# Two mixture-of-experts stages: how rows reach their expert's blocks, and who splits the weights

## What is computed

```python
w, sel = top_k(dist(y, centroid), 2)       # two experts for each token
w = softmax(w)
for e in range(8):
    h = silu(y @ Wg[e] + bg[e]) * (y @ W1[e] + b1[e])
    out += we[:, e:e+1] * (h @ W2[e] + b2[e])
```

## Time and profile before

| | |
|---|---|
| median of 3 runs | 1390.04 us (1389.5 to 1395.8) |
| the profiled execution | 1399.42 us |
| its span, first to last instruction | 1397.6 us, mean granted TensorE clock 0.809 |
| TensorE busy | 1033.1 us (74%) |
| VectorE busy | 731.0 us (52%) |
| ScalarE busy | 574.9 us (41%) |
| GpSimd busy | 429.5 us (31%) |

### The profile page before, as it was taken

How to read it: one execution, slowest core, us unless ns; L and a number is a source line. 1 busy time by engine, 2 the same in 40 slices (tenths; PEclk the granted TensorE clock), 3 DMA queues, 4 the chain that set the end, 5 groups by cost and what they waited for, 6 DMA issues and landing times. The chain is left out here.

```text
span 1397.6 us, 23299 instructions
## 1 busy us (share of the span) xinstructions
PE 1033.1 (74%) x7645; PEld 757.6 (54%) x7645; DVE 731.0 (52%) x1988; ACT 574.9 (41%) x1177; POOL 429.5 (31%) x462
## 2 busy tenths in 40 slices
PE   3899883569962787878665899999995556518990
PEld 2566553559951555554343566666663445418990
DVE  3467625466654656555253655655532455654553
ACT  1356532155532355445333354444441244324552
POOL 1144433513442111110143133333342241572332
PEclk9999965689985568775577899999997666658995
DMA  7111100111230111111030000111122430011113
GB/s 262 41 43 56 56 30 12 37 30 42 55 85 0 32 48 42 38 35 44 18 118 0 2 23 18 25 32 32 32 52 42 143 137 0 20 40 41 53 49 91
DMA packets 80293, 68.33 MB, mean 49 GB/s; under 512 B 6769, under 2 KB 72600, under 8 KB 79666
## 3 DMA queue, kind: packets, MB, share of 16 engines
q1 hardware_dynamic: 75666, 58.37, 14.6%
q0 software_dynamic: 4512, 8.47, 1.9%
HBM read 40.61 MB, written 26.59 MB: 48 GB/s over the span
## 5 line engine op out<-in xcount | busy, mean ns | idle before, releaser
L413 DVE TENSOR_REDUCE a_rowmax<-a_banks 128x4 f32<-128x1024 f32 (+1 forms) x112 | 137.0, 1223 | 109.4 <-PE a_banks L623 92.3
L507 ACT ACTIVATE a_probs<-a_banks 128x1024 f32<-128x1024 f32 x112 | 114.8, 1025 | 108.1 <-PE a_banks L609 88.6
L2133 POOL TENSOR_TENSOR a_both<-a_probs 128x512 f32<-128x512 f32 x64 | 81.8, 1278 | 193.5 <-ACT a_probs L2336 193.5
L1054 POOL DMA_INDIRECT acc<-m_result,m_yb x77 | 75.7, 983 | 156.3 <-DVE m_result L1346 82.0
L2336 ACT ACTIVATE a_probs<-a_banks 128x1024 f32<-128x1024 f32 x64 | 65.6, 1025 | 114.2 <-PE a_banks L2384 114.2
L2245 DVE TENSOR_REDUCE a_rowmax<-a_banks 128x4 f32<-128x1024 f32 x64 | 78.0, 1219 | 23.9 <-PE a_banks L2364 23.9
L1452 ACT ACTIVATE m_gate<-m_banks 128x352 f32<-128x352 f32 (+1 forms) x93 | 42.8, 460 | 104.8 <-PE m_banks L1639 87.3
L647 PE MATMUL a_banks<-a_probs,a_V 128*32 128x256 f32 x768 | 79.0, 495 | 5.6 <-ACT a_raw L500 4.9
L609 PE MATMUL a_banks<-a_QT,a_KT 25*128 25x256 f32 x384 | 59.6, 393 | 30.4 <-DVE a_rowmax L413 29.3
L1047 POOL DMA_INDIRECT rows<-m_yrow,m_idx x64 | 64.0, 1000 | 47.9 <-issue 22.9
L609 PEld LDWEIGHTS a_banks<-a_QT,a_KT 25*128 25x128 f32 x384 | 37.1, 232 | 67.9 <-issue 50.8
(11 more groups left out here) (347 smaller groups left out, 2854.7 us busy)
## 6 DMA issues: line engine op xcount, KB each, us to landing
rows<-fill SPq DMA_DIRECT2D x16, 520.0 KB, 4.6
a_factor<-recip_rows SPq DMA_DIRECT2D x32, 256.0 KB, 4.6
rows<-fill SPq DMA_DIRECT2D x15, 455.0 KB, 4.2
m_yb<-rows SPq DMA_DIRECT2D x77, 65.0 KB, 1.8
f_expert<-in_experts SPq DMA_DIRECT2D x16, 257.5 KB, 2.9
m_parts<-acc SPq DMA_DIRECT2D x16, 256.0 KB, 5.0
bias<-in_bias_zero SPq DMA_DIRECT2D x1, 3248.0 KB, 20.1
e_gu_lo<-in_gu SPq DMA_DIRECT2D x1, 2736.0 KB
```

The source lines that it names most:

```text
L413: nc.vector.reduce_max(o, src, AX).then_inc(rowmax_ready, 1)
L507: nc.scalar.activation(probs[h][:, k, :, :], ps[:, 4:6, :], ACT.Exp, scale=SCALE).then_inc(exp_done, 1)
L1054: nc.gpsimd.indirect_dma_start(acc.rearrange("k n d -> (k n) d"), bass.IndirectOffsetOnAxis(yb[b % YB][:, P:P + 1].bitcast(U32), 0), resul ...
L2133: nc.gpsimd.tensor_tensor(both[u % 4][:, :, :], p[:, :, 0, :], p[:, :, 1, :], ALU.add).then_inc(both_ready, 1)
```

## The change

`rows` is now laid out by partition and place: each token's normed row lies, once for each choice, where its tile has it, so SyncE stores them with 8 plain DMAs in each layer (2 for each run), and place 0 holds zeros. The fills in the attentions, the scatters of line 1047 and the loads of line 1006 are gone. A row has 129 words, without the place.

In their stead each block's list of pairs is worked out: VectorE finds each pair's block and its row in the block (`positions`), makes for each pair a one-hot row over the 128 rows of a block (`block_list`) and a product of its one-hot block with its own partition and place (`listed`), and TensorE multiplies and adds the two (32 small bfloat16 products, event `list`) so that each block's column holds, for each of its rows, the partition and the place of its pair. `indices` turns this into `idx` for gathers and `idx_out` for scatters (out of bounds where a block has no pair). The events `count`, `list` and `idx` take the place of `map`; in layer 0 they stand between slots 2 and 5, in layer 3 after the last run's routing.

GpSimd gathers each block by an indirect DMA (`gather`) and scatters its results as before. In slot r it first gathers item r + 5 (GA), with the wait that SyncE's loads had, then scatters item r-2. GpSimd also does the low parts of all split experts but layer 0's shared one, which VectorE keeps. In layer 0 the work items are now 10 shared tiles, the blocks with a shared tile after blocks 8, 17, 26 and 35, and 2 shared tiles; the splits come earlier in the events. `acc` has the layout of `rows`, so its loads read 4 rows of a partition in one run of 2 KB.

The diff, cut to its core:

```diff
-ROW = P + 2
+ROW = P + 1
+PLACES = 2 * TILES + 1
+NOWHERE = float(1 << 24)
...
+def shared_first_work(NB, lead, every, behind):
+
+    work = [("shared", t) for t in range(lead)]
+    t = lead
+    for b in range(NB):
+        work.append(("routed", b))
+        if b % every == every - 1 and t < TILES - behind:
+            work.append(("shared", t))
+            t += 1
+    return work + [("shared", u) for u in range(t, TILES)]
...
+             ("spot", 0), ("share", 0), ("split", 0), "slot", ("norm", 2), ("router", 2), ("one_hot", 1), ("split", 1), "slot",
+             ("score", 2), ("gap", 2), ("spot", 1), ("share", 1), ("split", 2), "slot", ("norm", 3), ("router", 3),
+             ("one_hot", 2), ("split", 3), "slot", ("score", 3), ("gap", 3), ("spot", 2), ("share", 2), ("one_hot", 3),
+             ("split", 4), "slot", ("spot", 3), ("share", 3), ("split", 5), ("split", 6), ("count", 0), "slot", ("list", 0),
+             ("list", 1), "slot", ("list", 2), ("list", 3), ("idx", 0)]
...
-    splits = {0: [0, 1, 2], 1: [3], 5: [4, 5], 6: [6, 7]}
+    splits = {0: [0, 1], 1: [2], 2: [3], 3: [4], 4: [5], 5: [6], 6: [7]}
...
-    events += [("send", RUNS - 1, 3), ("map", 0)]
+    events += [("count", 0)] + [("list", r) for r in range(RUNS)] + [("idx", 0)]
...
-    YB, RB = 8, 4
+    YB, RB, GA = 8, 4, 5
...
-            work = [("shared", t) for t in range(14)] + [("routed", b) for b in range(NB)] + [("shared", 14), ("shared", 15)]
+            work = shared_first_work(NB, 10, 9, 2)
...
-            sp.wait_ge(rows_sent, 16 * 2 * TILES)
-            sp.wait_ge(map_ready, 1)
-            own_wait(sp, st.sp_waited)
-            for b in range(NB):
-                n = sp.value_load(block_map[0:1, 1, b:b + 1], min_val=0, max_val=dispatch_rows(layer) // P - 1)
-                if b >= YB:
-                    sp.wait_ge(result_sent[(b - YB) % RB], 16 * ((b - YB) // RB + 1))
-                sp.dma_start(yb[b % YB][:, :], rows[n, :, :]).then_inc(block_loaded[b % YB], 16)
+            sp.dma_start(rows[:, 0, :], g.fill[:, :]).then_inc(rows_stored, 16)
+            for r in range(RUNS):
+                sp.wait_ge(copied, r + 1)
+                sp.wait_ge(share_ready, r + 1)
+                for k in range(2):
+                    first_place = 1 + k * TILES + r * RT
+                    sp.dma_start(rows[:, first_place:first_place + RT, :], yrow[k][:, tiles(r), :]).then_inc(rows_stored, 16)
             for k in range(RB):
                 sp.wait_ge(result_sent[k], 16 * len(range(k, NB, RB)))
             for r in range(RUNS):
                 for k in range(2):
-                    sp.dma_start(parts[r][:, k, :, :],
-                                 acc[k, r * RUN:(r + 1) * RUN, :].rearrange("(t p) d -> p t d", p=P)).then_inc(
-                        parts_loaded[r], 16)
+                    first_place = 1 + k * TILES + r * RT
+                    sp.dma_start(parts[r][:, k, :, :], acc[:, first_place:first_place + RT, :]).then_inc(parts_loaded[r], 16)
...
-            def send(r, some):
-                pool.wait_ge(idx_ready, r + 1)
-                pool.wait_ge(share_ready, r + 1)
-                pool.wait_ge(copied, r + 1)
-                pool.wait_ge(places_ready, 1)
-                pool.wait_ge(g.filled[layer], 16 * g.fill_parts)
-                for t in some:
-                    for k in range(2):
-                        c = (r * RT + t) * 2 + k
-                        nc.gpsimd.indirect_dma_start(rows.rearrange("n p c -> (n p) c"),
-                                                     bass.IndirectOffsetOnAxis(idx[:, c:c + 1], 0),
-                                                     yrow[k][:, r * RT + t, :], None).then_inc(rows_sent, 16)
+            def split(e):
+                n = split_at[e]
+                r = rows_of[2]
+                pool.wait_ge(hi_ready, n)
+                gu_hi, gu_lo, down = weights(e)
+                raw_gu, raw_full, raw_rest = raw(e)
+                nc.gpsimd.tensor_tensor(gu_lo, raw_gu, gu_hi.bitcast(F32), ALU.subtract)
+                nc.gpsimd.tensor_tensor(down[:, 0:2, 1, :], raw_full, down[:, 0:2, 0, :].bitcast(F32), ALU.subtract)
+                nc.gpsimd.tensor_tensor(down[0:r, 2, 1, :], raw_rest, down[0:r, 2, 0, :].bitcast(F32),
+                                        ALU.subtract).then_inc(split_ready, 1)
+
+            def gather(i):
+                b = routed(i)
+                if b is None:
+                    return
+                if b == 0:
+                    pool.wait_ge(idx_ready, 1)
+                    pool.wait_ge(rows_stored, 16 * (2 * RUNS + 1))
+                if b >= YB:
+                    pool.wait_ge(result_sent[(b - YB) % RB], 16 * ((b - YB) // RB + 1))
+                nc.gpsimd.indirect_dma_start(yb[b % YB][:, :], None, rows.rearrange("p t c -> (p t) c"),
+                                             bass.IndirectOffsetOnAxis(idx[:, b:b + 1], 0)).then_inc(block_loaded[b % YB], 16)
 
             def send_result(i):
                 b = routed(i)
+                if b is None:
+                    return
                 pool.wait_ge(result_ready, i + 1)
-                nc.gpsimd.indirect_dma_start(acc.rearrange("k n d -> (k n) d"),
-                                             bass.IndirectOffsetOnAxis(yb[b % YB][:, P:P + 1].bitcast(U32), 0),
-                                             result[b % RB][:, :], None, bounds_check=2 * TOKENS - 1,
+                if b == 0:
+                    pool.wait_ge(idx_ready, 2)
+                nc.gpsimd.indirect_dma_start(acc.rearrange("p t d -> (p t) d"),
+                                             bass.IndirectOffsetOnAxis(idx_out[:, b:b + 1], 0),
+                                             result[b % RB][:, :], None, bounds_check=P * PLACES - 1,
...
+            ahead = -1
...
+                if kind == "split" and r < NE - 1 + by_distance:
+                    split(r)
+                if kind == "slot":
+                    while ahead < r + GA:
+                        ahead += 1
+                        gather(ahead)
...
             def spots(r):
                 dve.wait_ge(rank_ps, r + 1)
-                if r == 0:
-                    dve.wait_ge(region_ready, 1)
                 rank = ranked.rearrange("p (g e) -> p g e", g=G)
                 steps.after(nc.vector.tensor_tensor(spot[:, :, :], rank,
-                                                    region[:, :].rearrange("p (o e) -> p o e", o=1).to_broadcast([P, G, NE]),
-                                                    ALU.add))
+                                                    one_hot[r].rearrange("p t c e -> p (t c) e"), ALU.mult))
                 steps.wait(dve)
-                steps.after(nc.vector.tensor_tensor(spot[:, :, :], spot[:, :, :],
-                                                    one_hot[r][:, :, :, :].rearrange("p t c e -> p (t c) e"), ALU.mult))
+                nc.vector.reduce_sum(rank_of[:, r * G:(r + 1) * G], spot[:, :, :], AX).then_inc(spot_ready, 1)
...
+            def positions():
 
                 dve.wait_ge(count_ps, 1)
-                then(nc.vector.tensor_tensor(
-                    more[:, :, :], counted[0:1, :].rearrange("p (e o) -> p e o", o=1).to_broadcast([1, NE, TILES]),
-                    limit_f[:, :].rearrange("p (o j) -> p o j", o=1).to_broadcast([1, NE, TILES]), ALU.is_gt))
+                dve.wait_ge(numbers_ready, 2)
+                then(nc.vector.tensor_tensor(more[:, :, :], over(counted, TILES), under(limit_f[:, :], NE), ALU.is_gt))
                 then(nc.vector.reduce_sum(count[:, :], more[:, :, :], AX))
-                io = at["iota"][0:1, :]
-                then(nc.vector.tensor_tensor(upto[:, :, :], io.rearrange("p (e o) -> p e o", o=1).to_broadcast([1, NE, NE]),
-                                             io.rearrange("p (o e) -> p o e", o=1).to_broadcast([1, NE, NE]), ALU.is_ge))
-                counts = count[:, :].rearrange("p (o e) -> p o e", o=1)
-                then(nc.vector.tensor_tensor(upto[:, :, :], upto[:, :, :], counts.to_broadcast([1, NE, NE]), ALU.mult))
+                then(nc.vector.tensor_tensor(upto[:, :, :], over(at["iota"], NE), under(at["iota"], NE), ALU.is_ge))
+                then(nc.vector.tensor_tensor(upto[:, :, :], upto[:, :, :], under(count[:, :], NE), ALU.mult))
                 then(nc.vector.reduce_sum(last_of[:, :], upto[:, :, :], AX))
-                then(nc.vector.tensor_tensor(past[:, :, :],
-                                             number_f[:, :].rearrange("p (b o) -> p b o", o=1).to_broadcast([1, NB, NE]),
-                                             last_of[:, :].rearrange("p (o e) -> p o e", o=1).to_broadcast([1, NB, NE]),
+                then(nc.vector.tensor_tensor(first[:, :], last_of[:, :], count[:, :], ALU.subtract))
+                then(nc.vector.tensor_tensor(first_of[:, :, :], one_hot_all[:, :, :, :, :].rearrange("p r t c e -> p (r t c) e"),
```

(45 more changed lines are left out.)

180 lines of the change are left out of this document (88 added, 92 removed).

## The result

The changed kernel took 1460.88 us (median of 4 runs, 1448.6 to 1462.89) against 1390.76 for the kernel before in the same session: a ratio of 1.0467 (95% interval 1.0424 to 1.051), slower as forecast, by more than forecast: 1426 with a range of 1398 to 1456. The median lies 5 us above the range; the ratio, put on the 1390.04 us that the forecast started from, gives 1455, 1 us inside it. The profiled execution took 1462.46 us, span 1460.8 against 1397.6: +63.2.

The account below looks back on a forecast made before the run. TensorE was taken to bound the routed parts, chains of small VectorE, ScalarE and GpSimd steps the routing parts. Terms 52.7 + 3 - 7 - 9 - 4 = +36 us on the 1390.0 median gave 1426 us, range 1398 to 1456.

Parts of the forecast that it names:

- the loop: Layer 3, GpSimd's queue: each gather waits for the scatter issued just before it, 4.36 us a block against 2.51.
- Layer 3, routed part, +52.7: Layer 3's 39 blocks: gathers waiting for scatter landings set the pace, so the part ends 52.7 us later.
- the 0.78 us from release to start: GpSimd, layer 3: an indirect DMA that has waited starts 0.78 us after its release; counted in each block's 4.36 us.
- The bound with 0.30 in its place, +31.4: Layer 3's routed part, low bound: landing 2.1 and start 0.30 after release give 3.68 us a block, +31.4 us.
- Layer 0, routed part, +3: Layer 0's blocks: tight gather waits only after shared tiles, mostly hidden by the lead of five items; +3 us, 0 to +10.
- rival 2: ScalarE's "remote" waits move to layer 0's routed part: one more 16 us, 1442 us; chance 0.09 together with rival 3.
- rival 3: GpSimd's splits stop VectorE outright, 40 us of them in place of 12: +20, 1446 us; chance 0.09 together with rival 2.
- Layer 0, routing part, -7: Layer 0 before item 10: 32 scatters and seven VectorE splits go, list work is added; -7 us, -18 to +10.
- The splits on GpSimd: Both routing parts: GpSimd's subtractions hold VectorE 0.54 us each, half of 45 counted, against 21 us of VectorE splits saved.
- Layer 3, routing part, -9: Layer 3 before the first block: ranks come earlier without queued scatters and three VectorE splits; -9 us, -18 to +5.
- Loads of `acc`, -4: First `acc` load of each stage, now in 2 KB runs: -2 us each, -4 in all (bounds -6, 0).
- The fills, 0: Attentions: 32 fills go, but no engine's wait names a DMA there, so 0 us (bound -3).

Follow-up runs that it names:

- session B: Kernel before (1375.7 us) and changed kernel, both unchanged, measured again on one chip with no remote waits: changed kernel 1.0362 of before.
- ahead4: Changed kernel with gathers 4 items ahead in place of 5 (GA = 4): 1.0137 of the kernel before.
- order: Changed kernel, but in a slot GpSimd issues the scatter first and then the gather: 1.0146 of the kernel before.
- deep: Changed kernel with 12 block buffers, 6 result buffers, gathers 8 items ahead (layer 0: from slot 5 on): 1.0016 of before, repeated on another chip 1.0457.
- mixed: Kernel before with `deep`'s layer 3, layer 3's `rows` and `acc` in the new layout, no fills in att1: 1.0180 of the kernel before.
- session A: Runs on one chip of the changed kernel with fewer items ahead or more buffers; kernel before 1378.2 us, no remote waits in the profiles.
- session D: Runs on another chip of `deep` unchanged (1.0457 of before) and with a GpSimd memset after each scatter (1.0422); kernel before 1394.8 us.

## Why the prediction was right in sign, and short in size

The direction and the main mechanism held. Against the forecast +36 in the profiled execution, +63.2 came. That the time came out so near the range is in part luck: the loop was priced 14 us too high, which hid half of the 27 us by which layer 0's routed part was priced too low. By the steps of the prediction (forecast: measured):

- **Layer 3, routed part, +52.7: +38.8** (+39.6 in session B). The mechanism is shown by `ahead4`, `order` and `deep`, each of which removes the loop in another way. The size was off by one term: the 0.78 us from release to start. The prediction calls it measured on the very instruction, but the row is a scatter's, and what waits here is a gather. The gather started 2.52 us after the scatter's start, about 0.2 us on top of the landing of 2.3. It is not the releaser that differs: the first gather, released by VectorE's indices, starts 0.30 us after their end (291.10 against 290.62 + 0.18), and the changed kernel's result scatters that waited for VectorE still took 0.76 to 0.81. In the trace a register move of the same line stands in front of the scatter and none in front of the gather; whether it makes the difference was not tried. The bound with 0.30 in its place, +31.4, was nearer. A round of 3.80 in place of 4.36 makes 30 x 0.56 = 17 us less; 3 came back elsewhere in the stretch.
- **Layer 0, routed part, +3: +30.1.** This step failed. Without stalls it is +5.1 (session B), GpSimd's saturation as forecast, and in bounds. The other 25 came only in the session with stalls, in which 21.8 us of ScalarE's waits in this part end on late signals from TensorE, while indirect DMAs follow each other at 0.30 us. That is rival 2, which was priced at 16 us and given, with rival 3, a chance of 0.09. The ground for doubting it, that layer 3's 32 scatters showed none, was true of the trace and too weak: the last twelve of them (1242.5 to 1256.6 us) fell almost wholly into the 18.48 us in which TensorE stood idle and had no end to signal, and before that at most four followed each other at 0.30 us. The prediction also took the presence of these waits for a property of the kernel.
- **Layer 0, routing part, -7: +2.3; +14.4 without stalls.** I read the 16.1 us of remote waits in the earlier trace rows as a cost of the 32 scatters and let the change remove them. This failed too, and without stalls it is the largest miss, 21 us. In the session that has them the kernel before loses 19.2 us (88.9 against 69.7) and the changed one still 7.1 (91.2 against 84.1), with its 8 gathers in a row. The rest is the chain: 23.4 us from the count to the indices against 16 worked out. `positions()` took 10.9 in place of 7.5, of which 3.8 are three small steps held by GpSimd's subtractions (1.33 + 0.65 + 2.38, against 0.22 + 0.22 + 0.17 unhindered); the list steps took 4.7 (4.9 forecast). Between the lists stands a second slot, which the sum leaves out: 1.8 us of VectorE's steps and 3.2 of waiting for ScalarE before them, whose products TensorE had taken up late.
- **The splits on GpSimd.** Rival 3's mechanism is in the timeline: the held steps end within 0.1 us of a subtraction's end. The Trainium skill (SBUF — State Buffer, "Who interferes with whom") says that a VectorE instruction with two SBUF inputs contends with a GpSimd instruction that reads SBUF, and the trace agrees: all three held steps (1.33, 0.65 and 2.38 us) have two. Rival 3 priced it at +20. It came to about what VectorE saves in layer 0, and less than that in layer 3: with the splits back on VectorE the routing parts together were 3 us longer, not shorter.
- **Layer 3, routing part, -9: -8.1** (-4.6 in session B). The size came out in the first session; in the later one it is half.
- **Loads of `acc`, -4: -0.7** in the two tails. The landing went from 5.0 to 4.5, not to 2.9.
- **The fills, 0: about -3.** Layers 1 and 2 took 3.5 and 2.8 us less; whether it is the missing fills was not tried alone.

The stretches of the first session add up: 2.3 + 30.1 - 0.1 - 3.5 - 8.1 + 38.8 - 0.6, and 4.2 by which the layer 0 stage happened to start later, give 63.1. The medians differ by 7 us more, because the profiled execution of before took longer than each of its timed runs.

No version beats the kernel before. `deep` equals it (0.9990 to 1.0043) in a session without stalls and loses 4.6% in one with them; `mixed`, run only in a session with stalls, loses 1.8%.

## What to carry to other kernels

A wait that costs nothing on one engine's queue can set the pace on another's: before moving it, write down the queue in order and ask whether the thing waited for stands directly in front; one instruction more between them, or one item less ahead, was worth 34 us here. Price the start after a wait by a row of the same kind of instruction: a result scatter started 0.76 to 0.81 us after its release, a gather 0.2 to 0.3. And a wait in the profile that no semaphore of the kernel explains should be looked for on a second chip before it is booked as a gain of the change.

## What was not expected of the hardware

Where indirect DMAs follow each other at 0.30 us, TensorE's semaphores can be raised late, and ScalarE starts late with them; whether it happens goes with the chip or the session. The same kernel took 1381.56 us in session A and 1457.74 in session D, with before at 1378.2 and 1394.8. Three of five sessions showed the waits, mostly of 1 to 3 us each in the routed parts; two showed none in eight profiles, and the medians of before fall in the same two groups (1391 to 1397, 1376 to 1378). The longest in the earlier trace rows, 12.5 us, counts all of ScalarE's idle time: the product it waited for ended at 276.52 us and ScalarE started at 283.47, so 7 us of it are the stall. VectorE, too, waited 2.7 us in that part for a signal of TensorE, raised 3.2 us after the product's end. The kernel before shows no stall in its routed parts, where its scatters stand 0.9 us or more apart. In the loop of layer 3 after the change, and beside the 32 scatters of layer 3 before it, indirect DMAs followed each other at 0.30 us mostly in twos while TensorE worked, and there was no stall either. How long a row must be was not tried, and by what way a DMA of GpSimd's delays TensorE's signal no row shows.

A gather lands in 2.6 us (2.5 to 3.9 over both stages) where a scatter takes 2.3. This is the landing of `deep`'s line 1074 in layer 0:

```profile
DMA to landing us min/median/max: 2.5/2.6/3.7
```
